# Scaling and splitting the second pair of heads on GpSimd beside VectorE, in the set-up of a graph network kernel

## What is computed

```
proj  = einsum('nf,hfg->nhg', x, w_proj)           # 4 heads
delta = proj[sender] - proj[receiver]
radial_logits     = <delta, radial_score> - scale * edge_len
tangential_logits = <delta, tangential_score>
out = softmax-weighted sums of delta over the edges of a receiver, for both kinds of logits
x = layernorm(x + (x + mean_over_heads(out) @ w_out))
```

## Time and profile before

| | us |
|---|---|
| runs | 2970.07 median of 3 (2968.24 to 2970.22) |
| profiled execution | 2972.75, its span 2970.9 |
| busy in the span | PE 2225.6, PEld 1710.1, DVE 2083.0, POOL 1783.2, ACT 631.7 |
| costliest line | L880 on POOL, 888 gathers, 862.8 busy and 290.2 idle before them |

### The profile page before, as it was taken

The page is one execution under the profiler, slowest core; times in us unless marked ns, Lnnn a source line. Parts: engine busy times, 40 slices in busy tenths (PEclk is TensorE's granted clock), DMA queues, the critical chain, the costliest instruction groups (busy, mean ns, idle before and its releaser), DMA issues. The chain is left out here.

```text
span 2970.9 us, 64636 instructions
## 1 busy us (share of the span) xinstructions
PE 2225.6 (75%) x13922; PEld 1710.1 (58%) x13923; DVE 2083.0 (70%) x7862; ACT 631.7 (21%) x1180; POOL 1783.2 (60%) x1857
## 2 busy tenths in 40 slices
PE   0288888889888898986799557667676676676748
PEld 0255555555555555555799446656566666565637
DVE  6477777777777777747566557777777777777755
ACT  0323322333222333231000111111111111111100
POOL 0077777777777777730001167777777777777722
PEclk9999999999999999985899555555555555555558
DMA  1144554545545455542000133333333333333330
GB/s 42 55 128 133 141 142 128 142 130 145 141 129 143 126 142 141 134 88 57 20 1 2 35 77 83 81 82 82 81 81 82 81 83 81 81 82 80 82 41 12
DMA packets 425511, 268.62 MB, mean 90 GB/s; under 512 B 334070, under 2 KB 375909, under 8 KB 425445
## 3 DMA queue, kind: packets, MB, share of 16 engines
q0 software_dynamic: 71040, 176.52, 23.6%
q1 hardware_dynamic: 284418, 49.42, 8.8%
q10 hardware_dynamic: 69986, 41.88, 4.6%
HBM read 231.16 MB, written 15.97 MB: 83 GB/s over the span
## 5 line engine op out<-in xcount | busy, mean ns | idle before, releaser
L880 POOL DMA_INDIRECT edges_rows<-table,edges_idx x888 | 862.8, 972 | 290.2 <-issue 221.9
L2066 POOL DMA_INDIRECT all_arena<-table_kv,edges_idx x888 | 855.8, 964 | 276.3 <-issue 255.7
L2258 PE MATMUL edges_acc<-edges_values,edges_into 128*128 128x136 f32 x1776 | 511.4, 461 | 259.7 <-DVE edges_values L2146 237.6
L2258 PEld LDWEIGHTS edges_acc<-edges_values,edges_into 128*128 128x128 f32 x1776 | 416.6, 328 | 307.0 <-DVE edges_values L2146 286.4
L1053 PE MATMUL edges_radial_ps<-edges_rows,edges_into_w 128*128 x1776 | 461.3, 396 | 94.1 <-SPq L897 75.3
L962 DVE TENSOR_SCALAR edges_cell<-edges_ramp,edges_strip_key,first_key 128x400 bf16<-128x400 f16 x1184 | 451.2, 381 | 0.0
L1053 PEld LDWEIGHTS edges_radial_ps<-edges_rows,edges_into_w 128*128 128x128 f32 x1776 | 319.8, 190 | 219.0 <-issue 178.0
L2111 DVE TENSOR_SCALAR edges_ahead<-edges_nodes,edges_starts,edges_dst_f 128x128 bf16<-128x128 f32 x894 | 261.7, 360 | 174.3 <-issue 174.3
L961 DVE TENSOR_SCALAR edges_low<-edges_places,first_src_low 128x128 bf16<-128x128 bf16 x1184 | 332.1, 281 | 0.0
L2192 ACT COPY edges_into_t<-edges_t_ps 128x384 bf16<-128x384 bf16 x298 | 142.9, 480 | 874.0 <-PE edges_t_ps L2226 865.1
L967 DVE TENSOR_SCALAR edges_into_w<-edges_nodes,first_dst_f,first_weight 128x128 f32<-128x128 f32 x888 | 276.1, 368 | 0.0
(11 more groups left out here) (343 smaller groups left out, 2561.4 us busy)
## 6 DMA issues: line engine op xcount, KB each, us to landing
edges_values<-in_edge_attr SPq DMA_DIRECT2D x888, 32.0 KB
all_arena<-all_arena ACTq DMA_DIRECT2D x50, 400.0 KB
edges_rows<-table,edges_idx POOLq DMA_INDIRECT x888
all_arena<-table_kv,edges_idx POOLq DMA_INDIRECT x888
edges_attr<-in_edge_attr ACTq DMA_DIRECT2D x51, 256.0 KB
edges_bias<-bias_kept SPq DMA_DIRECT2D x296, 12.0 KB
bias_kept<-edges_bias_out ACTq DMA_DIRECT2D x52, 64.0 KB
table<-all_arena SPq DMA_DIRECT2D x1, 3250.0 KB, 11.4
```

Of the source, the lines that this page charges most:

```text
L880: pool.indirect_dma_start(rows[:, n, :], None, table0, bass.IndirectOffsetOnAxis(ap=idx[:, n:n + 1], axis=0)).then_inc(s_rows[g], 16)
L2066: pool.indirect_dma_start(rows[:, n, :], None, table_kv, bass.IndirectOffsetOnAxis(ap=idx[:, n:n + 1], axis=0)).then_inc(s_rows[g], 16)
L2258: last = nc.tensor.matmul(acc[:, 0:2 * F + H2], into[:, h, j, :], values[:, h, j, :], start=False, stop=True, skip_group_check=True)
```

## The change

Two helper functions hold the scaling of a pair and one subtract. VectorE calls them for the first pair (k = 0), as before. GpSimd, behind its all-reduce, waits for the second exponential (`s_exp` at 2) and calls them for the second pair (k = 1). Each pair has semaphores of its own. ScalarE casts in each of three rounds the second pair first, then the first.

```diff
-                s_part, s_cast = ph.sem("s_scaled"), ph.sem("s_parts")
+                s_part, s_cast = [ph.sem(f"s_scaled{k}") for k in range(2)], [ph.sem(f"s_parts{k}") for k in range(2)]
+
+                def scale_pair(eng, k, done):
+                    for h in range(2):
+                        eng.tensor_tensor(scaled[:, k, :, h * F:(h + 1) * F], x_in[:, :, :], over(factor_t[:, :, 2 * k + h], F), ALU.mult)
+                    eng.tensor_copy(scaled[:, k, :, 2 * F:PAIR], factor_t[:, :, 2 * k:2 * k + 2])
+                    eng.memset(scaled[:, k, :, PAIR:TAN], 1.0).then_inc(done, 1)
+
+                def take_part(eng, k, n):
+                    eng.wait_ge(s_cast[k], n + 1)
+                    eng.tensor_tensor(scaled[:, k, :, :], scaled[:, k, :, :], head_part(k, n), ALU.subtract).then_inc(s_part[k], 1)
...
+                        pool.wait_ge(s_exp, 2)
+                        scale_pair(pool, 1, s_part[1])
+                        for n in range(2):
+                            take_part(pool, 1, n)
...
-                        for k in range(2):
-                            for h in range(2):
-                                dve.tensor_tensor(scaled[:, k, :, h * F:(h + 1) * F], x_in[:, :, :], over(factor_t[:, :, 2 * k + h], F), ALU.mult)
-                            dve.tensor_copy(scaled[:, k, :, 2 * F:PAIR], factor_t[:, :, 2 * k:2 * k + 2])
-                            dve.memset(scaled[:, k, :, PAIR:TAN], 1.0).then_inc(s_part, 1)
+                        scale_pair(dve, 0, s_part[0])
                         for n in range(2):
-                            for k in range(2):
-                                dve.wait_ge(s_cast, 2 * n + k + 1)
-                                dve.tensor_tensor(scaled[:, k, :, :], scaled[:, k, :, :], head_part(k, n), ALU.subtract).then_inc(s_part, 1)
-                        dve.memset(last_block[:, :, :], 0.0).then_inc(s_part, 1)
+                            take_part(dve, 0, n)
+                        dve.memset(last_block[:, :, :], 0.0)
...
                         for n in range(3):
-                            for k in range(2):
-                                act.wait_ge(s_part, 2 * n + k + 1)
-                                act.copy(head_part(k, n), scaled[:, k, :, :]).then_inc(s_cast, 1)
+                            for k in (1, 0):
+                                act.wait_ge(s_part[k], n + 1)
+                                act.copy(head_part(k, n), scaled[:, k, :, :]).then_inc(s_cast[k], 1)
```

## The result

The changed kernel takes 2977.72 us (median of 6 runs, 2974.5 to 2983.99), beside 2970.08 of the kernel before on the same chip: ratio 1.0027, 95% interval 1.0017 to 1.0037, so some 8 us slower. One of the six runs of the kernel before took 7149.23; without it the median is the same to 0.01. The forecast was 2974.1, with no measurable difference as its likeliest case. The time lies in the forecast's range, but outside its likeliest case. What the prediction worked out of the set-up and of the next stage's head came nearly as it said. A second term, of some 5 us, isn't in it at all: it arises in the 1150 us of gathers behind the set-up, which the change does not touch.

A forecast was written before the change was run, and what follows sets the result against it. GpSimd's gathers were taken as the bound, VectorE close behind. Set-up +9.8 and next stage -5.8 sum to +4.0 us, which on the median 2970.07 gives 2974.1; range 2967.5 to 2981.0.

The forecast's parts named there:

- Parts 1 and 5: GpSimd's code load moves behind the all-reduce: first multiply at 107.4 to 108.2, next stage's iota 6.9 earlier against block's end.
- Rival C: Next stage's head: load not saved, or TensorE's weights set the start; about 0.5 returns, +9.3 us, 2979.4; chance 0.10.
- Part 2: GpSimd's durations in the set-up: multiply 2.88 us, subtract 7.1 us, with 5.7 as the subtract's lower end.
- Rival B: Set-up: GpSimd costs more per element, 4.8 us more in all, +8.8, 2978.9; chance 0.19.
- rival E: Set-up: exclusion holds but GpSimd's subtract runs at the better operand rate (5.7): +1.2 us, 2971.3; chance 0.10.
- Part 3: Set-up: two-input operations of GpSimd and VectorE exclude each other, laid end to end less 0.13 us of start-up each.
- rival A: Set-up: no exclusion, the two engines' operations interleave: +0.1 us, 2970.2; chance 0.13.
- Part 4: The new set-up step by step: the block ends at 144.4 instead of 134.7, +9.8 us.
- Part 5: Next stage: the saved code load lets GpSimd's gathers start earlier, giving back 5.8 us, ends 4.7 and 6.9.
- The hold at the third side: Next stage's third side: GpSimd waits for VectorE's index, which holds its gain to 5.8 us.
- What is held at the third side is held to the end: Gather loop: the chain of gather, product and index closes on itself, so the 5.8 us gain lasts to the end.
- the other order of service: Set-up: VectorE always served first where both engines wait; block +11.6 us instead of +9.8, 1.8 more.

The follow-up runs named there:

- e1: The kernel before with one 128x1 addition on GpSimd behind the all-reduce, so only the code load moves: 2965.41 us, ratio 0.9970.
- e5: The changed kernel with a pair's copy and memset placed ahead of its two scaling multiplies: ratio 1.0020 to the kernel before.
- e4: The changed kernel measured once more, with nothing altered: 2985.75 us, ratio 1.0036 to the kernel before.
- e9: The changed kernel with six 128x1 memsets added behind VectorE's last set-up memset: 2971.81 us, ratio 1.0010 to the kernel before.
- e11: The changed kernel itself, unaltered, run beside e9: 2977.12 us, ratio 1.0032 to the kernel before.
- e12: The changed kernel with the second pair's subtracts given back to VectorE and four 128x1 memsets behind VectorE's set-up: ratio 0.9985 to the kernel before.
- e2: The changed kernel with a second all-reduce ending GpSimd's list in the block, so the iota needs its load again: 2985.98 us, ratio 1.0044.

## Why the prediction was right and wrong

**Code load (Parts 1 and 5).** Right: multiply at 107.63, forecast 107.4 to 108.2; no load at the iota; first gather 3.2 after the last cast's end, where it was 9.7. It is worth 6.6 us at the 43rd gather and 8.9 measured by itself (e1; its interval, 5.9 to 11.9, holds the 6.6). Rival C falls.

**GpSimd's durations (Part 2).** Multiply 2.88 forecast, 2.89 measured. Subtract 7.1 forecast, 6.15 measured with VectorE quiet: 1.88 ns an element, nearer the lower end (5.7) than the value taken. The Trainium skill (GPSIMD Engine Reference, section Performance versus the Vector engine) gave an estimate of 7.2 for it; this trace does not agree, and the row decides. Rival B falls, rival E is nearly met in its rate.

**Exclusion (Part 3).** Right, down to the 0.13; rival A falls. But it was laid on two-input operations alone. The step that failed is in Part 4: "VectorE's first scaling multiply, held, to 117.2", with the copies before it at nothing, and the same for the pair's copy. Each such copy is held by whatever GpSimd operation is running, 2.78 and 6.14. The first hold cost little, as it only took the place of the multiply's. By the rows it even let GpSimd's copy and memset through, so that the cast of pair 1 ended at 118.59 and not at 120.5. The second made pair 0's first part late: its cast started at 125.22, when the forecast had it done by 123.5. That cost 3.1: VectorE's first subtract starts at 128.20, and GpSimd's had ended at 125.10. The earlier cast of pair 1 (1.9) and GpSimd's two shorter subtracts (0.7 and 0.9) gave back about as much, and so the block's end, 144.20, agrees with 144.4 by luck, by a balance of errors; e5 takes the copy's part out, and the end moves to 141.14. The Trainium skill (SBUF — State Buffer, section Who interferes with whom) lets a copy contend with GpSimd when it runs in a mode that uses both ports. By the Trainium skill (VectorE: DVE Perf Modes, section Mode 2×_2P — use both read ports for one tensor) such a mode takes one source, both sides in SBUF. The trace agrees, for the copies held (2.78, 2.84, 6.14) and for the memset that is not (2.79); that the copies ran in such a mode, no run here shows.

**What comes back (Part 5).** Forecast -5.8, ends -4.7 and -6.9. At the 43rd gather the block's +9.5 to +9.9 has become +2.4 to +4.6 in the four profiles of the same set-up (changed, e4, e9, e11), so 5.1 to 7.1 came back. The hold at the third side was not as tight as it said in the profiled execution of the changed kernel; the size is right.

**"What is held at the third side is held to the end."** This sentence failed, and with it the size of the loss: +4.0 became +8. The 43rd gather is +2.4, the last +5.5, and in e4 +2.9 becomes +11.9. With the list's length restored, the same set-up measures +3.0 (e9), which is what the sum of +4.0 was for. The missing term is +5.3 (2977.12 less 2971.81), and the sum of the two, +8.3, agrees with the measured +8.0. That the time still lies in the forecast's range is luck: its upper end, 2981.0, was laid for rivals B and C, which fell, with the other order of service. Part 4 costed each instruction taken from VectorE by the time that it ran, and never asked what the ones behind it do when the list gets shorter.

**The better kernel.** The load alone (e1) beats both: 2965.41 beside 2973.99 of the kernel before, ratio 0.9970. Scaling moved as well, with the list kept at its length, gives 0.9985 (e12); nothing that moves arithmetic to GpSimd gave more than the load by itself.

## What to carry to other kernels

Here, half of a VectorE job was no gain on GpSimd while VectorE worked beside it: it ran at about 0.6 of the speed, one engine waited for the other for whole operations, and even VectorE's copies of 50 elements waited. What GpSimd's idle time is good for is its own code load: issue a one-element operation of the set that is needed next, as soon as the all-reduce is over. And where a long loop follows whose engines run close to each other's pace, test a change of a few us with the instruction lists padded to their old lengths before you believe its size or sign.

## What was not expected of the hardware

- VectorE's copy of 128x50 f32 elements takes 0.19 alone and 2.78, 2.84 or 6.14 beside an operation of GpSimd, until that ends. Its memset of 128x3275 elements was not held (2.79).
- GpSimd's load goes by what stands next in its list: a copy and a memset ran without one, and the load (7.45) began only behind them, not when the engine fell idle. All-reduce and iota each took one in turn in e2: 6.0 of idle time before the all-reduce, and a first gather 7.2 later than in the changed kernel.
- A gather's issue takes 0.95 or 1.17 us, in step with VectorE's half where it is long, and that can hold for several halves. The length of VectorE's list ahead of the loop changed how often, from 3 to 15 long gathers to 25 to 74, worth 5.3 us here.
- A pause of 0.12 us on VectorE stands at one place of its instruction list and moves with it: six records on in a list six shorter, ten back in a list ten longer, in each of 24 windows.
